# A recurrent-and-attention layer on one core: second-stage products put in another order on TensorE, the output norm's weight folded into the projection

## What is computed

```python
def step(h, inp):                       # the state-space scan inside s
    x_t, dt_t, B_t, C_t = inp
    dA = jnp.exp(dt_t * A)
    h = h * dA[:, :, None, None] + (dt_t[:, :, None] * x_t)[..., None] * B_t[:, None, None, :]
    y = jnp.einsum('bhpn,bn->bhp', h, C_t)
    return (h, y)
...
y = y * jax.nn.silu(z)
y = y * jax.lax.rsqrt(jnp.mean(jnp.square(y), axis=-1, keepdims=True) + EPS) * norm_w
return y @ out_proj_w.T                 # then residual, norm, a gelu block, residual
...
scores = jnp.einsum('bhqd,bhkd->bhqk', q, k) * HD ** (-0.5)      # inside g: 16 heads of 8
attn = jax.nn.softmax(jnp.where(causal[None, None], scores, -jnp.inf), axis=-1)
ao = jnp.einsum('bhqk,bhkd->bhqd', attn, v).transpose(0, 2, 1, 3).reshape(B, T, C) @ wo.T
...                                     # then four experts, two of them chosen per token
x = x + s * g
```

## Time and profile before

| what | value |
|---|---|
| median of 3 runs (lowest to highest) | 864.25 us (862.42 to 871.44) |
| the profiled execution's own time; its span | 864.34 us; 862.6 us |
| granted TensorE clock, mean over the span | 0.993 |
| busy PE / DVE / ACT / POOL | 91% / 71% / 58% / 37% of the span |
| ScalarE's exponentials (L1099) | 192, 165.9 us busy, 129.7 us idle before them |
| period of the loop (start of group 1, one pass to the next) | 100.9 us, of which stage_a from there to its end 30.57 us |

### The profile page before, as it was taken

How to read it: one execution, slowest core, us unless ns; L and a number is a source line. 1 busy time by engine, 2 the same in 40 slices (tenths; PEclk the granted TensorE clock), 3 DMA queues, 4 the chain that set the end, 5 groups by cost and what they waited for, 6 DMA issues and landing times. The chain is left out here.

```text
span 862.6 us, 18148 instructions
## 1 busy us (share of the span) xinstructions
PE 788.2 (91%) x5472; PEld 483.5 (56%) x5472; DVE 610.4 (71%) x1467; ACT 502.4 (58%) x960; POOL 318.7 (37%) x600
## 2 busy tenths in 40 slices
PE   2779999999999989999999999999999998999897
PEld 1455564756556555655647565475556556475555
DVE  2786479784888758785697848877587866968534
ACT  2435784467753776457844677537765577446652
POOL 5424534053512617045340534226260362505400
PEclk9998999999999999999999999999999999999999
DMA  4000000000000000000000000001000000000000
GB/s 166 2 8 14 14 2 1 9 16 25 0 8 12 26 0 0 8 13 25 0 0 8 14 24 0 2 14 30 1 0 8 12 26 0 0 8 14 25 1 13
DMA packets 15145, 11.73 MB, mean 14 GB/s; under 512 B 1040, under 2 KB 13968, under 8 KB 14992
## 3 DMA queue, kind: packets, MB, share of 16 engines
q1 hardware_dynamic: 15120, 11.43, 4.4%
HBM read 7.76 MB, written 2.10 MB: 11 GB/s over the span
## 5 line engine op out<-in xcount | busy, mean ns | idle before, releaser
L1099 ACT ACTIVATE sb_pr<-S 128x768 f32<-128x768 f32 (+1 forms) x192 | 165.9, 891 | 129.7 <-PE S L444 129.7
L1196 DVE TENSOR_REDUCE sb_mx<-S 128x2 f32<-128x256 f32 (+3 forms) x256 | 198.0, 817 | 29.7 <-PE S L444 29.3
L1716 POOL TENSOR_SCALAR_AFFINE_SELECT sb_pr<-sb_pr 128x256 f32<-128x256 f32 (+1 forms) x192 | 98.9, 517 | 322.2 <-ACT sb_pr L1099 319.7
L444 PE MATMUL R<-sb_pr,sb_va 128*32 128x512 f32 (+3 forms) x1024 | 89.5, 444 | 0.0
L444 PE MATMUL R<-sb_W,sb_pr 128*128 128x96 f32 (+1 forms) x512 | 69.5, 276 | 0.0
L444 PE MATMUL R<-sb_xfT,sb_W 128*128 128x512 f32 x144 | 69.2, 602 | 0.0
L444 PE MATMUL S<-sb_kT,sb_qT 32*128 32x256 f32 (+3 forms) x512 | 56.3, 384 | 13.7 <-DVE sb_mx L1196 10.0
L444 PEld LDWEIGHTS R<-sb_W,sb_pr 128*128 128x128 f32 x512 | 63.5, 192 | 3.8 <-issue 3.5
L444 PEld LDWEIGHTS S<-sb_kT,sb_qT 32*128 32x128 f32 x512 | 27.5, 183 | 66.3 <-DVE sb_mx L1196 58.6
L444 PE MATMUL S<-sb_qT,sb_kT 32*128 32x256 f32 (+3 forms) x512 | 56.3, 384 | 5.7 <-ACT sb_pr L1099 4.9
L1430 DVE SCALAR_TENSOR_TENSOR sb_x<-R,sb_wts,sb_x 128x96 f32<-128x96 f32 x128 | 40.6, 317 | 22.8 <-PE R L444 19.4
(11 more groups left out here) (216 smaller groups left out, 1735.6 us busy)
## 6 DMA issues: line engine op xcount, KB each, us to landing
sb_xin<-x SPq DMA_DIRECT2D x9, 256.0 KB, 2.7
sb_W<-weights SPq DMA_DIRECT2D x1, 2290.0 KB, 11.0
sb_qT<-sb_mT SPq DMA_DIRECT2D x128, 4.0 KB
sb_xres<-x SPq DMA_DIRECT2D x8, 256.0 KB, 2.8
out<-sb_xres SPq DMA_DIRECT2D x7, 256.0 KB, 2.3
sb_cT<-sb_xact SPq DMA_DIRECT2D x8, 128.0 KB, 2.3
sb_W<-weights SPq DMA_DIRECT2D x1, 514.0 KB, 5.8
sb_cst<-consts SPq DMA_DIRECT2D x1, 328.0 KB, 3.1
```

The costliest lines, as they stand in the source:

```text
L444: return pe.matmul(o, lhsT, rhs, start=start, stop=stop, skip_group_check=True)
L1099: act.activation(pr[:, e % 4, :, 0:n], S[pair_of_exp(e)][:, :, 0:n], ACT.Exp).then_inc(p_sb, 1)
L1196: o = dve.tensor_reduce(mx[:, n // P - 1, g, heads[0]:heads[1] + 1], found[:, :, at_col:at_col + n], AX.X, ALU.max, negate=True)
L1716: pool.affine_select(out=keep, in_=keep, compare_op=ALU.is_ge, fill=0.0, base=0, pattern=pattern, channel_multiplier=-1)\
```

## The change

The products of stage_a stand in another order. In a group, each `weigh_values` now follows the scores directly (u = 0, 2, 4) and the full-array products follow it together: `turn_y`, (in group 1 `turn_maxima`), `segments` at u = 0; `turn_values`, `scan_inputs` at u = 2; `scan_outputs`, `new_state` at u = 4. Group 0 keeps its order. `prep_a` goes to the end of group 3. `turn_maxima` of the second pair goes through R[3] in place of R[1], and so waits for `yz_sb` where it waited for `seg_sb`. The wait for `wm_sb` goes from the head of `scan_outputs` to just ahead of the products that read `wm`. ScalarE's, VectorE's and GpSimd's lists follow: `evac_values` changes place with `evac_y`, `es` goes from u = 1 to u = 3, `square_y` to u = 5; VectorE's `values` goes to u = 2, ahead of `scan_products`, `scan_weights` to u = 3, the statistics of the next input and two join steps one place later; GpSimd's `xw` goes from u = 2 to u = 3. The weight of the output norm is multiplied into the projection weights by VectorE once, ahead of the loop, and `evac_y` is one instruction without a scale.

```diff
-SIGMOID_AT = {5: (0, 1, 2), 9: (3, 4)}
-JOIN_AT = {11: (0, 1), 15: (2,)}
+SIGMOID_AT = {5: (0, 1, 2), 11: (3, 4)}
+JOIN_AT = {15: (0, 1), 17: (2,)}
-STATS_AT = 8
+STATS_AT = 9
...
             def turn_maxima(r, pair, o):
                 if pair:
-                    pe.wait_ge(seg_sb, at(seg_sb, r, 2))
+                    pe.wait_ge(yz_sb, at(yz_sb, r, 1))
...
             def turn_values(r, g):
+                if g == 0:
+                    pe.wait_ge(mT_sb, at(mT_sb, r, 2))
...
             def scan_outputs(r, c):
-                pe.wait_ge(wm_sb, at(wm_sb, r, c + 1))
                 pe.wait_ge(xdt_sb, at(xdt_sb, r, c + 1))
...
                     mm(R[3][:, n * P:(n + 1) * P], xact[:, n, s], diag_d[:, n, :], c == 0 and n == 0, False)
+                pe.wait_ge(wm_sb, at(wm_sb, r, c + 1))
...
-                    if u == 0 and g > 0:
-                        turn_y(r, g - 1)
-                    if u == 1 and g > 0:
-                        weigh_values(r, e - 3)
-                        segments(r, g)
-                        scan_inputs(r, g)
                     if e == 2:
                         segments(r, 0)
-                    if u == 3:
-                        weigh_values(r, e - 3)
-                        if g >= 1:
-                            turn_values(r, g - 1)
+                    if u == 0 and g > 0:
+                        weigh_values(r, e - 2)
+                        turn_y(r, g - 1)
+                        if g == 1:
+                            turn_maxima(r, 1, R[3])
+                        segments(r, g)
+                    if g == 0 and u == 3:
+                        weigh_values(r, 0)
+                    if u == 2 and g > 0:
+                        weigh_values(r, e - 2)
+                        turn_values(r, g - 1)
+                        scan_inputs(r, g)
                     if u == 4:
+                        if g > 0:
+                            weigh_values(r, e - 2)
                         scan_outputs(r, g)
-                    if u == 5:
-                        if g < T - 1:
+                        if g == T - 1:
+                            prep_a(r)
+                        elif g > 0:
                             new_state(r, g)
-                        weigh_values(r, e - 3)
-                    if (g, u) == (1, 2):
-                        turn_maxima(r, 1, R[1])
-                    if (g, u) == (3, 3):
-                        prep_a(r)
+                    if g == 0 and u == 5:
+                        new_state(r, 0)
+                        weigh_values(r, 2)
...
-                for n in range(2):
-                    i = act.activation(yT[:, n, c * P:(c + 1) * P], R[2][:, n * P:(n + 1) * P], ACT.Copy,
-                                       scale=vec[:, V_NORM + n:V_NORM + n + 1])
-                i.then_inc(yT_sb, 1)
+                act.activation(yT[:, :, c * P:(c + 1) * P], R[2][:, 0:DI].rearrange("p (n t) -> p n t", n=2),
+                               ACT.Copy).then_inc(yT_sb, 1)
...
                     if u == 0 and g > 0:
+                        evac_values(r, g - 1)
+                    if u == 1 and g > 0:
                         evac_y(r, g - 1)
-                    if u == 1 and g > 0:
-                        evac_values(r, g - 1)
-                    if u == (2 if g == 0 else 1):
+                        if g == 1:
+                            evac_maxima(r, 1, R[3])
+                    if u == (2 if g == 0 else 3):
...
+            for n in range(2):
+                ts(w2("op", D)[:, n, :], w2("op", D)[:, n, :], vcol(V_NORM + n), None,
+                   ALU.mult).then_inc(op_scaled, 1)
```

More of the change, by code:

```diff
@@ L231, in build @@
         wt_loaded = signal("wt_loaded", 0)
+        op_scaled = signal("op_scaled", 0)
         x_loaded = signal("x_loaded", 16, 1)
@@ L617, in new_state @@
                 pe.wait_ge(seg_sb, at(seg_sb, r, c + 1))
-                if c == 1:
-                    pe.wait_ge(mT_sb, at(mT_sb, r, 2))
                 mm(R[1][0:NS, 0:DI], btok[:, c % 2, :], xw[:, c % 2, :]).then_inc(hn_ps, 1)
@@ L904, in _ @@
             pe.wait_ge(wt_loaded, 16)
+            pe.wait_ge(op_scaled, 2)
             with pe.Fori(0, B - 1) as r:
@@ L1135, in stage_a @@
                                        ACT.Exp).then_inc(seg_sb, 1)
-                    if u == 1 and g > 0:
+                    if u == 5 and g > 0:
                         square_y(r, g - 1)
-                    if (g, u) == (1, 2):
-                        evac_maxima(r, 1, R[1])
                     if e == 3 and tail:
                         negative_exp(r)
-                    if (g, u) == (3, 3):
+                    if (g, u) == (3, 5):
                         evac_a(r)
@@ L1519, in stage_a @@
                             split_maxima(r, MAX_AT[e] // UNITS)
-                    if u == 1:
+                    if u == 2 and g >= 1:
+                        values(r, g - 1, ot_ps, ao_sb)
+                    if u == (2 if g else 1):
                         scan_products(r, g)
-                    if u == 2:
+                    if u == (3 if g else 2):
                         scan_weights(r, g)
-                    if u == 3 and g >= 1:
-                        values(r, g - 1, ot_ps, ao_sb)
                     if u == 5 and g < T - 1:
@@ L1562, in _ @@
             stage_b(-1, False, True)
+            dve.wait_ge(wt_loaded, 16)
+            for n in range(2):
+                ts(w2("op", D)[:, n, :], w2("op", D)[:, n, :], vcol(V_NORM + n), None,
+                   ALU.mult).then_inc(op_scaled, 1)
             stage_a(-1, False)
@@ L1718, in stage_a @@
                         .then_inc(pm_sb, 1)
-                    if u == 2 and g < T - 1:
+                    if u == (3 if g else 2) and g < T - 1:
                         pool.wait_ge(xdt_sb, at(xdt_sb, r, g + 1))
```

## The result

The changed kernel takes 869.4 us (median of 20 runs, 868.5 to 870.8); the kernel before, run beside it, 864.2 us (20 runs, 862.4 to 871.7). The ratio is 1.0046, with a 95% interval of 1.0027 to 1.0064: some 4 us slower by that ratio, 5 by the medians, where the prediction said 862, a little faster. The profiled execution has a span of 867.1 us against 862.6. TensorE's busy time hardly moved; VectorE's and GpSimd's rose, by 7.6 and 5.2 us, although the change gives VectorE two instructions more and GpSimd none.

The account below looks back on a forecast made before the run. TensorE, busy 91%, bounded the kernel, in stage_a looping with ScalarE. Groups of -0.87, -0.10 and +0.68 us gave -0.29 a stage_a, -2.3 in eight; plus 0.2 for weight scaling, 864.34 became 862.2, said as 862; range 853 to 870.

Parts of the forecast that it names:

- S0 to S2: First interval, a group's first scores to its second: ScalarE becomes the bound, 3.04 us in place of 3.20.
- S4 to S0: Third interval, a group's third scores to the next group's first: same products in another order, 3.65 us.
- the last stretch: End of group 3, third scores to projection: 5.76 us in place of 4.98, wait for yz about 1.0.
- C1: A group's first weigh_values (256+128 columns): claimed not to wait for GpSimd's mask, ready 6.1 us after preceding group's second scores.
- My 0.05: TensorE's change from row tiles straight to column tiles, scores to weigh_values: taken as 0.05 us, between 0 and 0.13.
- Slack elsewhere: GpSimd's and VectorE's work in stage_a: masks ready in time; yz and state have about 0.35 us in hand.
- three signs of being wrong: End stretch staying at 5.0; segments waiting for state beyond first scores + 1.7 us; C1 waiting for a mask.
- Other: Rival: GpSimd's masks late, or a first stage or stage_b that reacts; no time given; chance 0.08.
- Slower, VectorE's list: Rival, VectorE ahead of scan_combine: yz and state 1 us later cost up to 10 us, 870; chance 0.16.
- The fold: Output norm's weight multiplied into projection weights, one yT copy instead of two: costed at 0, uncovered 0.1 a stage.
- fewer changes of form: TensorE in stage_a: grouping products saves three tiling changes, 0.3 us a stage_a, 2.3 in eight, if nothing else moved.
- P: Theory from the experiments: VectorE's joins and GpSimd's rs and masks, all reading SBUF, hold each other up, costing 1.02 us.

Follow-up runs that it names:

- e8: e2 with ScalarE's copy of oT moved behind the group's second exponential; 856.4 us, ratio 0.9891 to the kernel before.
- e4: The kernel before with only the scaled projection weights and one yT copy per chunk in place of two; 859.8 us, ratio 0.9933.
- e2: The changed kernel with VectorE's last two reciprocals where the two joins stood, and the joins behind the last exponentials; 862.1 us, ratio 0.9953.
- e7: The changed kernel without the scaled projection weights, so with two scaled yT copies again; 870.7 us, ratio 1.0053 to the kernel before.
- e1: The changed kernel with VectorE's first two joins three steps earlier, at step 12 in place of 15; 868.2 us, ratio 1.0013 to the kernel before.

## Why the prediction was wrong

**What held.** All that was worked out of TensorE and ScalarE. S0 to S2 is 3.04 with TensorE waiting for an exponential in group 2; C2 starts 0.58 after S2; the waits for `es` and `ao` are gone; S4 to S0 is 3.65 in both groups; the last stretch is 5.73 or 5.74 for 5.76, with 0.99 of wait for `yz`. Group 1 came out right in the sum by compensation: I had TensorE bound its first interval with 3.1, but ScalarE did with 3.04; TensorE's own work there is 2.88, as e8 shows, so the 0.15 for changes of form was too much. The rule of the Trainium skill (TensorEngine Tiling (Array Packing), Key Properties) that I weighed, that every change of tiling mode drains TensorE, doesn't show at the new steps: S0 to C1 takes 0.43 us (389.19 to 389.62), as S0 to `turn_y` did, and S4 to C3 0.39 (394.93 to 395.32), where S4 to the full-array product of `hst` takes 0.38 in e4. My 0.05 was, if anything, too much.

**The step that failed** is "Slack elsewhere", the overlap of VectorE's and GpSimd's work, whose cost it put at nothing. It laid out GpSimd's list with `rs` at 1.03 and the masks at 1.22, as the earlier trace rows have them, and got C1's mask 6.1 us after S2, "so C1 doesn't wait". It came 7.48 after (392.22 to 399.70): 0.46 more for `rs`, 0.91 more for the masks. The durations were those of a place where no instruction of VectorE with two inputs in SBUF lay over them (but `yz`, over the masks' last 0.1). The order showed that the joins would stand there; the step never asked what lies beside them. Its second half, the state 1.67 after S0, came out at 2.64 (398.59 to 401.23) for the same reason. Where the joins are taken away (e2; `rs` keeps its 1.49), C1 doesn't wait, the state comes 1.77 after S0 (398.23 to 400.00), and the wait for it is 0.17 where I had said 0.15. Two of the three signs of being wrong that the prediction names came true: `segments` wait beyond S0+1.7, and C1 waits for a mask. GpSimd's late masks it had only under "Other", at 0.08 together with two more causes. The measured 869.4 lies inside its range of 853 to 870 only because that range takes in most of the slower rival.

The kernel before had the warning, in a row that I had left out of the earlier trace rows. GpSimd there, a mask of 256 columns under the second join (VectorE, 390.71 to 391.40); the next one, with nothing of VectorE's two-input work over it, is the 0.41 of the earlier trace rows:

```profile
390.89 0.78 POOL L1716 TENSOR_SCALAR_AFFINE_SELECT sb_pr<-sb_pr 128x256 f32<-128x256 f32 x1 [1.56 <-ACT sb_pr L1099]
```

**The rival** "Slower, VectorE's list" had the place and the sign, and nearly the time (870), but not the mechanism: a list that is longer than that of the undisturbed joins, of other instructions, costs nothing (e2). "It decides from a delay of 0.35" was right; it was measured against undisturbed joins, which by e2 would have kept within it. VectorE's list did get longer, by 1.1 us (396.64 to 399.12 for two joins of 1.37), but through the collision.

**The fold** was costed at 0, which is what it is worth in the new order (e7). But the reason given looked only at the end of group 3. That it is worth 0.56 us a stage without the reordering (e4) stands nowhere in the prediction. By the traces, a stage_a goes from 30.57 to 30.01 with the fold, to 30.28 when the order is changed too and the joins kept apart (group 1 gains 0.64, group 2 loses 0.15, group 3 0.74), and to 31.30 with the joins where the change puts them. So "fewer changes of form" is a loss of 0.27 against the fold alone: what group 1 gains, the uncovered `yz` at the end of group 3 and ScalarE's copy between the exponentials take back.

**Still open.** I didn't try the fold alone with ScalarE's copy moved as in e8, so whether the old order or the new one is the better ground for it isn't settled. Nor is the 0.17 us settled by which the last stretch grows in e4: the `yz` instruction lies there over a mask of GpSimd and takes 0.62 instead of 0.45, which fits P but was only read, not tried. And no run takes only the masks or only the joins out of the collision, so what each of the two delays costs alone is an estimate.

## What to carry to other kernels

A duration from a trace holds for what lay beside it. When a change moves an instruction of VectorE or GpSimd, look what it will now lie over on the other of the two: if VectorE's has two inputs in SBUF and GpSimd's reads SBUF, expect one to wait for the other, as an estimate for the rest of its duration, or put there an instruction with one input. And cost each part of a change alone as well as in company: a part that is free in the new order may have been a gain in the old.

## What the runs showed of the chip that I had not expected

VectorE and GpSimd take turns. A join of 0.68 us took 1.52 over `rs` and a mask, `rs` 1.49 instead of 1.03 under `wm`, two masks 2.13 instead of 1.22 under the joins, and steps of four elements 0.63 and 0.72 instead of 0.20 (e1), since they wait for the rest of a long instruction on the other engine though they are short themselves. Two reciprocals of 128x128 (one input) over the same `rs` and masks changed nothing (e2). The Trainium skill (SBUF — State Buffer, Who interferes with whom) states this rule: "only the shared port pair causes contention, and it's an exclusive lock"; an instruction of VectorE with two inputs in SBUF contends with one of GpSimd that reads SBUF, and one with at most one such input, outside the modes that use both ports, doesn't. The traces agree in all these rows. One kind of row doesn't fit an engine that is blocked for as long as the other's instruction lasts: in the changed kernel GpSimd's norm step runs from 399.67 for 1.64 us, and VectorE's `yz` (400.03) and `hdec` (400.37), each with two inputs in SBUF, take their usual 0.42 and 0.41 under it, in every pass. What sets that step apart no run shows; it works on 8 elements a partition, the masks on 256.

TensorE's granted clock fell to half, 1.2 of 2.4 GHz, for a short stretch, once in some passes of the loop and not in others. Busy time by stretches in e1 (columns: stretch; its length; busy PE, PEld, DVE, ACT, POOL with counts; granted clock; DMA share and GB/s):

```profile
215.00:221.50 6.50, 4.92 (x25) 2.92 (x23) 6.20 (x16) 5.22 (x20) 0.68 (x1) 1.00 0.00 0
221.50:225.00 3.50, 3.46 (x19) 3.37 (x19) 2.15 (x8) 2.94 (x8) 2.06 (x5) 0.60 0.00 0
...
223.00:224.00 1.00, 1.00 (x7) 1.00 (x6) 0.15 (x1) 1.00 (x3) 0.85 (x3) 0.50 0.00 0
```

The clock falls behind a stretch in which TensorE was busy 4.92 of 6.50 us, and at the same place of the pass each time it does (in e1 at 222, 324, 426 and 730 us; in the kernel before at 525), but not in each pass: in the pass of e1 from 483 on the same stretch has the same 4.92 of 6.50 and the clock stays at 1.00. A pass with the low clock in it is 1.35 us longer (102.23 us against 100.88 in the kernel before). So executions of one kernel differ: the kernel before had a span of 860.8 us at a mean clock of 0.996 and of 870.1 at 0.980. That scatter is larger than what was looked for here, while the intervals between starts repeat to about 0.02 us; I didn't try what fills that stretch.
